# A four-layer kernel whose set-up is put in a new order: adapter rows made by full-array matmuls, first gates on ScalarE's queue, x loads and stores on SyncE

## The chip, the cores and the metric

The kernel runs on one core of a Trainium2 chip. TensorE (PE) multiplies, VectorE (DVE), ScalarE (ACT) and GpSimd (POOL) do elementwise work, SyncE (SP) only issues DMAs. The metric is the device time of one execution in microseconds. All matrices outside the recurrence are float32; the recurrent weights and state are split into two float16 parts.

## The reference

Four residual layers on x of 8 x 512 tokens of 256 channels, conditioned on 8 vectors of 256, each `x = x + layer(x)`:

```
L0: shared expert silu(x sw1') * (x sw3') @ sw2', plus 8 experts gelu(x rw1') @ rw2' weighted by the
    top-2 gates of sigmoid(x router' + cond router_t'), the sum / 3
L1: Haar transform, gated by g(cond); equals x + g * x per channel
L2: adapter: c = layernorm(cond); h = gelu(c W1 + b1); w = h W2 + b2 -> a1, b1, a2, b2, each (8, 256, rank 8)
    mid = gelu(x base_down + (x a2) b2');  out = mid base_up' + (mid b1) a1';  x + out
L3: GRU over 512 steps: Z, R = sigmoid(..), H~ = tanh(xh + (R*H) Whh'), H = Z H + (1-Z) H~, Y = H Whq'
```

W2 is 256 x 8192, 8 MB, half of all that is loaded.

## The kernel before

Tokens are time-major: a block is 16 time steps of 8 batches, 128 tokens, and there are 32 blocks. Activations lie with channels on the partitions. The loop (`blocks(body)`) runs over blocks; in block m it does the 16 recurrent steps of m, and between the steps' matmuls it places pieces of other blocks' work: output projection of m-1, layers 1 and 2 of m+1, layer 0 of m+2, the router of m+3 (`between_z_h`, `between_steps` on TensorE, `early`, `late` on VectorE, `after` on ScalarE). Every engine runs its own program in written order, and semaphores order the engines against each other. No scheduler has a say.

A block's gates go from token rows to a broadcast over partitions through DRAM: VectorE's 14 `gate_op`s end in `comb_rows`; SyncE's `spread_gates` writes them to `gates_dram` and loads them back to all partitions (`gates`); VectorE multiplies the experts' GELUs by them (`times_gate`), and TensorE's `l0_out` on `ge` and `rw2` follows. GpSimd computes the router's exponential (`exp_scores`), loads x (`load_x`, released by `x1_done`) and stores the output (`store`).

Before the loop, layer 0 of blocks 0 and 1, the router of 0 to 2 and layers 1 and 2 of block 0 must be done; this is the set-up. In TensorE's program it is: small products of cond, scores, `l0_whole_a` of block 0 (sw1, sw3, rw1), two matmuls for the scales of the recurrent weights, `l0_whole_b` of block 0 (sw2, rw2, which waits for the gates), the adapter, `l0_whole_a` of block 1, scores of block 2, then the chain of layer 2 of block 0 (`mid_base`, `low_in_rank`, `mid_low`, `up_base`, `up_low`), its projection into the gate banks (`project`), and `l0_whole_b` of block 1.

The adapter: `ah` (8 columns per half of the channels) stands in the array and W2 streams in 16 chunks of 512 columns to 8 rows of a bank; VectorE copies each chunk to `wrow`, and after each four chunks SyncE sends 8 DMAs that lay them out as `low`, (batch, rank) on 64 partitions, four such tiles: a2, b1, b2, a1. Biases are added, a2 and b1 are transposed to `a2b1`.

SyncE issues all weight loads in one row of code (L251 to L279), and only behind them `spread_gates(0)`.

## Time and profile before

| | us |
|---|---|
| median of 3 runs | 1319.07 (1315.98 to 1319.58) |
| the profiled execution | 1319.18 |
| its span | 1317.3 |
| TensorE busy | 1236.6 (94%) |
| VectorE busy | 898.1 (68%) |
| ScalarE, GpSimd busy | 444.5, 120.1 |
| first loop matmul starts | 121.96 |

The span is the stretch from the first to the last recorded instruction; the profiled execution's own time is 1.9 us more. Busy shares are means over set-up and loop, which have different limits. In the trace a float32 matmul is recorded as two instructions, and all matmuls have one line, L389, so they are told apart by tiles: `aw` is W2 (and W1 of the adapter), `rw` the routed experts or the router, `sw` the shared expert, `bank` one of four PSUM banks. SPq and POOLq are the engines' DMA issues. PEclk is the clock that TensorE was granted, 1.00 for 2.4 GHz and 0.50 for 1.2 GHz.

### The profile page before, as it was taken

The numbers are of one execution on the slowest core, as the hardware profiler recorded it, in microseconds if no ns is written. First come the engines' busy times: TensorE is split into PE (matmuls) and PEld (weight loads), VectorE is DVE, ScalarE is ACT, GpSimd is POOL, SyncE is SP. The second block draws the span as 40 slices with busy tenths as digits, with TensorE's granted clock in tenths as the row PEclk, the third lists the DMA queues.
The fourth block names the chain that finished last, engine by engine and source line by source line (L and its number), as shares of the span: only waits on it lengthen the run. The fifth ranks groups of instructions, "written<-read, shape, count | busy, mean of one in ns | idle before, by whom it ended". The sixth has DMA issues, their size and how long they took to land.

```text
span 1317.3 us, 53620 instructions
## 1 busy us (share of the span) xinstructions
PE 1236.6 (94%) x22255; PEld 1182.9 (90%) x22256; DVE 898.1 (68%) x5787; ACT 444.5 (34%) x2246; POOL 120.1 (9%) x120
## 2 busy tenths in 40 slices
PE   6387999999999999999999999999999999999975
PEld 6237999999999999999999999999999999999864
DVE  3243777777777777777777777777777777777555
ACT  1001333333333333333333333333333333333322
POOL 2410000000000000000000000000000000000000
PEclk9697999999999999999999999999999999999755
DMA  9411000011011001010111100111101100100000
GB/s 346 161 25 22 16 15 27 27 27 27 27 27 27 24 7 26 28 27 27 27 27 27 25 5 27 27 28 27 27 27 27 27 7 23 28 27 23 6 6 6
DMA packets 30325, 45.14 MB, mean 34 GB/s; under 512 B 8040, under 2 KB 24880, under 8 KB 28800
## 3 DMA queue, kind: packets, MB, share of 16 engines
q1 hardware_dynamic: 26784, 32.72, 8.7%
q0 software_dynamic: 3296, 8.98, 2.0%
q8 instruction: 174, 2.85, 0.9%
q14 instruction: 71, 0.58, 0.1%
HBM read 36.71 MB, written 4.72 MB: 31 GB/s over the span
## 4 chain that ended last, share of the span: by engine, by line
PE 88%; DVE 5%; SPq 3%; ACT 1%; issue 1%; DMA 1%; POOL 0%; DVEq 0%
PE bank L389 46%; PE gate_rh L389 31%; PE gate_z L389 10%; DVE state L984 1%; ACT rg L712 1%; DVE rhp L968 1%; DMA gates_t<-comb_rows 1%; DVE comb L842 1%; SPq L278 1%; DVE scaled L840 1%; DVE comb_rows L846 0%; SPq L271 0%; SPq L277 0%; DMA gates<-gates_t 0%; ACT hin L712 0%
## 5 line engine op out<-in xcount | busy, mean ns | idle before, releaser
L389 PEld LDWEIGHTS gate_rh<-state,whp 128*128 128x128 f16 x6144 | 233.6, 97 | 46.3 <-DVE state L984 34.3
L389 PE MATMUL gate_rh<-state,whp 128*128 128x8 f16 x6144 | 248.5, 167 | 26.7 <-DVE state L984 26.5
L712 ACT ACTIVATE rg<-gate_rh 128x16 f32<-128x16 f32 x512 | 94.2, 184 | 487.6 <-PE gate_rh L389 487.6
L389 PEld LDWEIGHTS gate_rh<-rhp,whp 128*128 128x128 f16 x6144 | 231.4, 97 | 16.2 <-DVE rhp L968 10.4
L389 PE MATMUL gate_rh<-rhp,whp 128*128 128x8 f16 x6144 | 236.6, 167 | 7.4 <-DVE rhp L968 7.4
L968 DVE SCALAR_TENSOR_TENSOR rhp<-rg,hist 128x16 f16<-128x16 f32 x512 | 89.6, 175 | 185.1 <-ACT rg L712 181.9
L389 PE MATMUL bank<-ge,rw 128*128 128x128 f32 x1024 | 165.4, 292 | 19.9 <-DVE ge L870 19.9
L389 PE MATMUL gate_z<-state,whp 128*128 128x16 f16 x4096 | 180.5, 177 | 0.0
L389 PE MATMUL bank<-xt,rw 128*128 128x128 f32 x1024 | 160.8, 292 | 6.7 <-DVE sa L851 4.8
L712 ACT ACTIVATE zg<-zsum 128x16 f32<-128x16 f32 x512 | 110.6, 216 | 166.3 <-DVE zsum L973 166.3
L978 DVE TENSOR_SCALAR zin<-zg,nsscale 128x16 f32<-128x16 f32 x512 | 124.6, 243 | 58.1 <-ACT zg L712 43.5
L984 DVE TENSOR_TENSOR_SCAN state<-zin,hin 128x32 f16<-128x32 f32 x512 | 115.1, 225 | 57.5 <-ACT hin L712 5.0
L389 PE MATMUL bank<-xt,sw 128*128 128x128 f32 x1024 | 153.6, 290 | 0.0
L389 PEld LDWEIGHTS bank<-ge,rw 128*128 128x128 f32 x1024 | 132.3, 193 | 20.1 <-DVE ge L870 20.1
L389 PEld LDWEIGHTS gate_z<-state,whp 128*128 128x128 f16 x4096 | 139.2, 96 | 0.0
L389 PEld LDWEIGHTS bank<-xt,rw 128*128 128x128 f32 x1024 | 129.8, 193 | 7.2 <-DVE sa L851 5.2
L712 ACT ACTIVATE hin<-gate_rh 128x16 f32<-128x16 f32 x512 | 95.4, 186 | 110.0 <-PE gate_rh L389 110.0
L389 PEld LDWEIGHTS bank<-xt,sw 128*128 128x128 f32 x1024 | 127.8, 194 | 0.1
L712 ACT ACTIVATE halved<-hist 128x16 f32<-128x16 f32 x512 | 106.3, 208 | 0.0
L988 DVE TENSOR_TENSOR state<-hist,state 128x16 f16<-128x16 f32 x512 | 92.1, 180 | 17.8
L986 DVE TENSOR_TENSOR_SCAN hist<-zin,hin 128x32 f32<-128x32 f32 x512 | 102.0, 199 | 1.0 <-issue 1.0
L973 DVE TENSOR_REDUCE zsum<-gate_z 128x16 f32<-128x32 f32 x512 | 93.6, 183 | 0.0
(155 smaller groups left out, 1636.5 us busy)
## 6 DMA issues: line engine op xcount, KB each, us to landing
gates<-gates_t SPq DMA_DIRECT2D x32, 512.0 KB, 5.3
aw<-in_aw SPq DMA_DIRECT2D x4, 2048.0 KB, 19.9
xt<-in_xT POOLq DMA_DIRECT2D x32, 128.0 KB, 5.6
out<-osb POOLq DMA_DIRECT2D x32, 128.0 KB, 3.6
rw<-in_rw SPq DMA_DIRECT2D x2, 1024.0 KB, 11.9
sw<-in_sw SPq DMA_DIRECT2D x3, 512.0 KB, 8.3
wh<-in_wh SPq DMA_DIRECT2D x3, 256.0 KB, 9.4
wx<-in_wx SPq DMA_DIRECT2D x3, 256.0 KB, 18.9
```

Source lines behind the costliest of these rows:

```text
L278: sp.dma_start(wq[:], a["wq"]).then_inc(wq_in, 16)
L389: return pe.matmul(o, w, x, start=start, stop=stop, skip_group_check=True)
L712: return act.activation(o, i, f, **kw)
L840: i = dve.tensor_scalar(scaled[:], ssel[:], den[:, 2:3], den[:, 1:2], ALU.mult, ALU.mult)
L842: i = dve.scalar_tensor_tensor(comb[:, 0:EXPERTS], chosen[:], den[:, 3:4], scaled[:], ALU.mult, ALU.add)
L968: dve.scalar_tensor_tensor(rhp[:, :, 0], rg[:], 1.0, old, ALU.add, ALU.mult).then_inc(rh_hi, 1)
L973: dve.tensor_reduce(zsum[:], z_now.rearrange("p a k c -> p k c a"), AX_X, ALU.add).then_inc(zsum_done, 1)
L978: dve.tensor_scalar(zin[:, :, :, 1], zg[:], -1.0, nsscale[:], ALU.add, ALU.mult)
L984: dve.tensor_tensor_scan(flat(state[:]), flat(zin[:]), flat(hin[:]), 0.0, ALU.mult, ALU.add)\
L986: dve.tensor_tensor_scan(flat(new), flat(zin[:]), flat(hin[:]), 0.0, ALU.mult, ALU.add).then_inc(st_all, 1)
L988: dve.tensor_tensor(state[:, :, :, 0], new[:, :, :, 1], state[:, :, :, 1], ALU.subtract).then_inc(st_low, 1)
```

## The change

The adapter's four tiles become two pairs (by index in W2: 2 with 1, that is a2 with b1, and 3 with 0, b2 with a1), each on 128 partitions: 64 rows of one, 64 of the other. `ah` is now a wide tile of zeros with the 8 columns in its middle. For rank r of slot s a window of 128 columns is taken in which the 8 columns stand at rows (8 s + r) * 8 of the output, and 16 ranks x 2 halves of K accumulate in one bank: the rows come out in place, with rank in the outer and batch in the inner position. `wrow`, its copies and the 32 DMAs go. `own` (the mask that keeps each token's own batch) and the bias follow the new layout, and `a2b1` is one transposed tile for both a2 and b1; `um` uses its lower 64 rows, `vm` its upper.

TensorE's order in the set-up is new. First the scores and the sw1 product, before the small products; the first adapter pair before block 0's expert output; all of block 1's layer 0 before layer 2 of block 0; the second pair within that chain. GpSimd's scaling of wx moves ahead of wqh, the exponentials of blocks 1 and 2 are placed among this work.

ScalarE issues the two gate DMAs of blocks 0 and 1. SyncE loads weights in a new order, starts with x of blocks 0 and 1, and takes over the later x loads and the stores; GpSimd keeps only the exponentials in the loop.

TensorE's program from the scales to the adapter (`gs`, `ge` and `sw`, `rw` are the expert output, `aw` and `ah` the adapter), before:

```order
L389 MATMUL gate_z<-peakd,ones 128x4 [waits peaks_dve]
L389 MATMUL bank<-gs,sw 128x128 [waits gs_done,setup_act]
L389 MATMUL bank<-gs,sw 128x128 x7
L389 MATMUL bank<-ge,rw 128x128 [waits ge47_done]
L389 MATMUL bank<-ge,rw 128x128 x7
L389 MATMUL bank<-ge,rw 128x128 [waits ge03_done]
L389 MATMUL bank<-ge,rw 128x128 x7
L389 MATMUL gate_rh<-aw,ah 8x512 [waits ad2_in2,scales_done]
```

and of the change:

```order
L379 MATMUL gate_z<-peakd,ones 128x4 [waits peaks_dve]
L379 MATMUL gate_rh<-aw,ah 128x256 [waits ad2_in2,zeroed]
L379 MATMUL gate_rh<-aw,ah 128x256 x15
L379 MATMUL gate_rh<-aw,ah 128x256 [waits ad2_in1]
L379 MATMUL gate_rh<-aw,ah 128x256 x15
L379 MATMUL bank<-gs,sw 128x128 [waits l0o_in,gs_done]
L379 MATMUL bank<-gs,sw 128x128 x7
L379 MATMUL bank<-ge,rw 128x128 [waits ge47_done]
L379 MATMUL bank<-ge,rw 128x128 x7
L379 MATMUL bank<-ge,rw 128x128 [waits ge03_done]
L379 MATMUL bank<-ge,rw 128x128 x7
```

Half of the adapter now stands ahead of the matmuls that wait for the gates (`ge47_done`, `ge03_done`).

TensorE's program at the start of layer 2 of block 0 (`x,down` is `mid_base`, `x,a2b` is `low_in_rank`), before:

```order
L389 MATMUL bank<-rw,xt 128x8 [waits x_in0,pe47_done]
L389 MATMUL bank<-rw,xt 128x8
L389 MATMUL gate_rh<-ident,low 128x64 [waits ready_dve]
L389 MATMUL gate_rh<-ident,low 128x64 x3
L389 MATMUL gate_rh<-zeros 128x512 [waits zeroed,ready_dve]
L389 MATMUL gate_rh<-zeros 128x512
L389 MATMUL gate_z<-zeros 128x512 x2
L389 MATMUL bank<-x,down 128x128 [waits x2_done,l2_in]
L389 MATMUL bank<-x,down 128x128 x3
L389 MATMUL bank<-x,a2b 128x128 [waits ready_dve]
```

and of the change:

```order
L379 MATMUL bank<-rw,xt 128x8 [waits x_in0,pe47_done]
L379 MATMUL bank<-rw,xt 128x8
L379 MATMUL bank<-x,down 128x128 [waits x2_done,x1_done,l2_in]
L379 MATMUL bank<-x,down 128x128 x3
L379 MATMUL bank<-x,a2b 128x128 [waits ready_dve]
L379 MATMUL bank<-x,a2b 128x128
L379 MATMUL gate_z<-aw,ah 128x256 [waits ad2_in3]
L379 MATMUL gate_z<-aw,ah 128x256 x15
L379 MATMUL gate_z<-aw,ah 128x256 [waits ad2_in0]
L379 MATMUL gate_z<-aw,ah 128x256 x15
L379 MATMUL bank<-um,low 128x128 [waits um_done,low_dve]
```

The transposes and the clearing of the banks leave this place, the second pair enters it.

SyncE's program in a block of the loop, before:

```order
L285 DMA gates_t<-comb_rows 128x32 [waits gates_in,gating]
L290 DMA gates<-gates_t 128x4x256 [waits ge03_done,ge47_done,comb_out]
L285 DMA gates_t<-comb_rows 128x32 [waits gates_in,gating]
L290 DMA gates<-gates_t 128x4x256 [waits ge03_done,ge47_done,comb_out]
```

and of the change:

```order
L299 DMA gates_t<-comb_rows 128x32 [waits gates_in,gating]
L303 DMA gates<-gates_t 128x4x256 [waits ge03_done,ge47_done,comb_out]
L253 DMA xt<-in_xT 128x2x128 [waits x1_done]
L294 DMA out<-osb 256x1x128 [waits out_done]
L299 DMA gates_t<-comb_rows 128x32 [waits gates_in,gating]
L303 DMA gates<-gates_t 128x4x256 [waits ge03_done,ge47_done,comb_out]
```

The x load now stands behind the gates broadcast of the block before in the same queue.

The diff, cut to its core:

```diff
-LOW_ORDER = (2, 1, 3, 0)
+PAIRS = ((2, 1), (3, 0))
+SPAN = 128
...
-        spare = (gate_rh[0], gate_z[0], gate_rh[1])
+        pair_ps = (gate_rh[1][:, 0:D], gate_z[1][:, 0:D])
...
-        score_ps = E47[:, KC * TOK:KC * TOK + EXPERTS]
+        score_ps = (E47[:, KC * TOK:KC * TOK + EXPERTS], gate_z[0][:, 0:EXPERTS])
...
         @block.sync
         def _(sp):
+            def load_x(m, par):
+                at = token_start(m)
+                sp.dma_start(xt[:, par], a["xT"][:, :, at:at + TOK]).then_inc(x_in[par], 16)
+
+            def load_aw2(i):
+                columns = slice(i * RANK * D, (i + 1) * RANK * D)
+                sp.dma_start(aw2[:, :, columns], a["aw2"][:, :, columns]).then_inc(ad2_in[i], 16)
...
             sp.dma_start(rw[:], a["rw"]).then_inc(l0_in, 16)
+            load_x((0, 0), 0)
+            load_x((0, 1), 1)
+            sp.dma_start(sw1[:], a["sw1"]).then_inc(l0w_in, 16)
             sp.dma_start(lnab[:], a["lnab"]).then_inc(ad_in, 16)
             sp.dma_start(aw1[:], a["aw1"]).then_inc(ad_in, 16)
-            sp.dma_start(sw1[:], a["sw1"]).then_inc(l0w_in, 16)
-            sp.dma_start(sw3[:], a["sw3"]).then_inc(l0w_in, 16)
-            sp.dma_start(rw1[:], a["rw1"]).then_inc(l0r_in, 16)
-            sp.dma_start(sw2[:], a["sw2"]).then_inc(l0r_in, 16)
-            sp.dma_start(rw2[:], a["rw2"]).then_inc(l0r_in, 16)
+            sp.dma_start(sw3[:], a["sw3"]).then_inc(l0w3_in, 16)
             sp.dma_start(iota[:], a["iota"]).then_inc(const_in, 16)
             sp.dma_start(rbias[:], a["rbias"].partition_broadcast(P)).then_inc(const_in, 16)
-            sp.dma_start(own[:], a["own"]).then_inc(const_in, 16)
+            sp.dma_start(rw1[:], a["rw1"]).then_inc(l0r_in, 16)
...
-            for i in LOW_ORDER:
-                columns = slice(i * RANK * D, (i + 1) * RANK * D)
-                sp.dma_start(aw2[:, :, columns], a["aw2"][:, :, columns]).then_inc(ad2_in[i], 16)
-            for b in range(B):
-                sp.dma_start(abias[b * RANK:(b + 1) * RANK], a["abias"]).then_inc(abias_in, 16)
+            load_aw2(2)
+            sp.dma_start(sw2[:], a["sw2"]).then_inc(l0o_in, 16)
+            sp.dma_start(rw2[:], a["rw2"]).then_inc(l0o_in, 16)
+            load_aw2(1)
+            sp.dma_start(abias[:], a["abias"]).then_inc(abias_in, 16)
+            sp.dma_start(own[:], a["own"]).then_inc(own_in, 16)
             sp.dma_start(down[:], a["down"]).then_inc(l2_in, 16)
             sp.dma_start(up[:], a["up"]).then_inc(l2_in, 16)
+            load_aw2(3)
+            load_aw2(0)
...
+            def store(m):
+                at = token_start(m)
+                sp.wait_ge(out_done, count(m, 1))
+                sp.dma_start(out[:, :, at:at + TOK], osb[:]).then_inc(stored, 16)
+
             def spread_gates(r):
                 sp.wait_ge(gating, GATE_OPS * (r + 1))
-                if r > 0:
-                    sp.wait_ge(gates_in, 16 * r)
+                sp.wait_ge(gates_in, 16 * r)
                 sp.dma_start(gates_dram, comb_rows[:]).then_inc(comb_out, 16)
                 sp.wait_ge(comb_out, 16 * (r + 1))
-                if r > 0:
-                    sp.wait_ge(ge47_done, r)
-                    sp.wait_ge(ge03_done, r)
+                sp.wait_ge(ge47_done, r)
+                sp.wait_ge(ge03_done, r)
                 sp.dma_start(gates[:], gates_dram.rearrange("(q e) j -> q e j", q=QUADS)[:, 0:EXPERTS]
                              .partition_broadcast(P)).then_inc(gates_in, 16)
 
-            spread_gates(0)
-            for at, i in enumerate(LOW_ORDER):
-                sp.wait_ge(wrow_dve, 4 * (at + 1))
-                for b in range(B):
-                    src = wrow[b:b + 1, at % 2].rearrange("b (r d) -> b r d", r=RANK)
-                    sp.dma_start(low[b * RANK:(b + 1) * RANK, i, :], src).then_inc(low_in[i], 16)
-
-            for r in range(1, BLOCKS):
-                spread_gates(r)
+            sp.wait_ge(x1_done, 1)
+            load_x((0, 2), 0)
+
+            def body(m, par, has_y, has_l23, has_l0, has_router):
+                if m[1] == 0:
+                    spread_gates(2)
+                if has_router:
+                    sp.wait_ge(x1_done, count(later(m, 1), 1))
+                    load_x(later(m, 3), 1 - par)
+                if has_y:
+                    store(later(m, -1))
+                if has_router:
+                    spread_gates(m[1] + 3)
+
+            blocks(body)
+            store((0, BLOCKS - 1))
+            sp.wait_ge(stored, 16 * BLOCKS)
...
         @block.gpsimd
...
+            pool.memset(ah[:], 0.0).then_inc(zeroed, 1)
...
+            pool.wait_ge(gating, 1)
+            exp_scores((0, 1))
...
+            pool.wait_ge(wx_in, 16 * 3)
+            for g in (R, Z, H):
+                pool.tensor_scalar(wx[:, g], wx[:, g], xscale[:, g:g + 1], None, ALU.mult).then_inc(wx_scaled, 1)
+            pool.wait_ge(gating, GATE_OPS + 1)
+            exp_scores((0, 2))
...
-            pool.wait_ge(x1_done, 1)
-            load_x(2 * TOK, 0)
-            exp_scores((0, 1))
-            exp_scores((0, 2))
-
             def body(m, par, has_y, has_l23, has_l0, has_router):
-                if has_l0 and not (type(m[0]) is int and m[1] + 3 >= BLOCKS):
-
-                    x_block = xcols(later(m, 3))
-                    pool.wait_ge(x1_done, count(later(m, 1), 1))
-                    load_x(x_block, 1 - par)
-                if has_y:
-                    store(later(m, -1))
                 if has_router:
                     exp_scores(later(m, 3))
...
+            def experts_up(m, par):
+                pe.wait_ge(l0r_in, 16)
+                pe.wait_ge(score_in, 2)
...
+            def adapt(p):
+                for slot in range(2):
+                    pe.wait_ge(ad2_in[PAIRS[p][slot]], 16)
+                    for r in range(RANK):
+                        for k in range(KC):
+                            at = (PAIRS[p][slot] * RANK + r) * D
+                            lead = SPAN - B - (slot * RANK + r) * B
+                            i = mm(pair_ps[p], ah[:, k, lead:lead + SPAN], aw2[:, k, at:at + D],
+                                   slot == 0 and r == 0 and k == 0, slot == 1 and r == RANK - 1 and k == KC - 1)
+                i.then_inc(adapt_pe, 1)
...
+            scores((0, 0), 0)
+            pe.wait_ge(ready_dve, 2)
+            shared_up((0, 0), 0)
+            scores((0, 1), 1, 1)
...
+            gated_up((0, 0), 0)
+            experts_up((0, 0), 0)
...
-            pe.wait_ge(setup_act, 2)
-            l0_whole_b((0, 0), 0)
-
-            pe.wait_ge(scales_done, 1)
-            for c in range(ADAPT // 512):
-                if c % 4 == 0:
-                    pe.wait_ge(ad2_in[LOW_ORDER[c // 4]], 16)
-                if c >= 3:
-                    pe.wait_ge(wrow_dve, c - 2)
-                at = LOW_ORDER[c // 4] * RANK * D + c % 4 * 512
-                for k in range(KC):
-                    i = mm(spare[c % 3][0:B, :], ah[:, k], aw2[:, k, at:at + 512], k == 0, k == KC - 1)
-                i.then_inc(adapt_pe, 1)
-            l0_whole_a((0, 1), 1)
+            pe.wait_ge(zeroed, 4)
+            adapt(0)
+            l0_whole_b((0, 0))
+            pe.wait_ge(low_dve, 1)
+            for k in range(KC):
+                i = mm(gate_rh[0][:, k * P:(k + 1) * P], low[:, 0, k * P:(k + 1) * P], ident[:], True, True)
+            i.then_inc(lowT_pe, 1)
+
+            shared_up((0, 1), 1)
+            gated_up((0, 1), 1)
+            experts_up((0, 1), 1)
+            l0_whole_b((0, 1))
             pe.wait_ge(pe47_done, 2)
             scores((0, 2), 0)
 
+            m0 = (0, 0)
+            pe.wait_ge(l2_in, 32)
+            pe.wait_ge(x1_done, 2)
+            mid_base(m0)
             pe.wait_ge(ready_dve, 4)
...
+            low_in_rank(x2, u_done)
+            adapt(1)
+            pe.wait_ge(low_dve, 2)
+            mid_low(m0)
             for t in (*gate_rh, *gate_z):
                 i = mm(t[:, :], zeros[:, 0:P], zeros[:], True, True)
             i.then_inc(bits_set, 1)
-            pe.wait_ge(l2_in, 32)
-            mid_base(m0)
-            pe.wait_ge(ready_dve, 5)
-            low_in_rank(0, x2, u_done)
-            mid_low(m0)
             up_base(m0)
-            low_in_rank(1, g2, v_done)
+            low_in_rank(g2, v_done)
...
-            l0_whole_b((0, 1), 1)
-            pe.wait_ge(split_w, 6)
+            pe.wait_ge(split_w, 5)
...
+            def comb_to_dram(r):
+                act.wait_ge(gating, GATE_OPS * (r + 1))
+                if r > 0:
+                    act.wait_ge(gates_in, 16 * r)
+                act.dma_start(gates_dram, comb_rows[:]).then_inc(comb_out, 16)
...
+            def gates_to_all(r):
+                act.wait_ge(comb_out, 16 * (r + 1))
+                if r > 0:
+                    act.wait_ge(ge47_done, r)
+                    act.wait_ge(ge03_done, r)
+                act.dma_start(gates[:], gates_dram.rearrange("(q e) j -> q e j", q=QUADS)[:, 0:EXPERTS]
+                              .partition_broadcast(P)).then_inc(gates_in, 16)
...
             gelu_experts(m0, 1, E47, ex47_done, pe47_done)
+            comb_to_dram(0)
             gelu_experts(m0, 0, A1, ex03_done, pe03_done)
+            gates_to_all(0)
+            comb_to_dram(1)
+            gates_to_all(1)
             tanh_a1(m1)
...
+            gelu_mid(m0)
             act.wait_ge(biases, 3)
             act.wait_ge(bits_set, 1)
             seed_rh(0)
             seed_z(0)
-            gelu_mid(m0)
...
+            def add_low_bias(p):
+                dve.wait_ge(adapt_pe, p + 1)
+                dve.tensor_tensor(low[:, p], pair_ps[p], abias[:, p], ALU.add).then_inc(low_dve, 1)
...
-            l0_whole_a(m0)
+            dve.wait_ge(score_exp, 1)
+            add_router_bias(m1, 1)
+            dve.wait_ge(const_in, 16 * 2)
+            gates_whole(m0)
+            silu_a1(m0)
+            times_a3(m0)
             find_scales()
...
-            l0_whole_b(m0)
+            gates_whole(m1)
+            times_gate(m0, 1, pe47_done, ge47_done)
+            times_gate(m0, 0, pe03_done, ge03_done)
+            dve.wait_ge(abias_in, 16)
+            add_low_bias(0)
             finish_l0(m0, 0)
             l1(m0)
-            for c in range(ADAPT // 512):
-                dve.wait_ge(adapt_pe, c + 1)
-                if c >= 8 and c % 4 == 0:
-                    dve.wait_ge(low_in[LOW_ORDER[c // 4 - 2]], B * 16)
-                dve.tensor_copy(wrow[:, c // 4 % 2, c % 4 * 512:(c % 4 + 1) * 512], spare[c % 3][0:B, :])\
-                   .then_inc(wrow_dve, 1)
-            l0_whole_a(m1)
+            dve.wait_ge(lowT_pe, 1)
+            dve.tensor_copy(a2b1[:].rearrange("p k c -> p (k c)"), gate_rh[0][:, 0:KC * P]).then_inc(ready_dve, 1)
+            silu_a1(m1)
+            times_a3(m1)
+            times_gate(m1, 1, pe47_done, ge47_done)
+            times_gate(m1, 0, pe03_done, ge03_done)
+            finish_l0(m1, 1)
             add_router_bias((0, 2))
             gates_whole((0, 2))
-            for i in LOW_ORDER:
-                dve.wait_ge(low_in[i], B * 16)
-            dve.wait_ge(abias_in, 16 * B)
-            dve.tensor_tensor(low[0:BR], low[0:BR], abias[:], ALU.add).then_inc(ready_dve, 1)
-            dve.wait_ge(lowT_pe, 1)
-            dve.tensor_copy(a2b1[:, :, :, 0:BR], gate_rh[0][:, 0:2 * KC * BR].rearrange("p (i k c) -> p i k c", i=2, k=KC))\
-               .then_inc(ready_dve, 1)
-            keep_own(m0, um, u_done, um_done)
-            keep_own(m0, vm, v_done, vm_done)
+            dve.wait_ge(own_in, 16)
+            keep_own(m0, um, slice(0, BR), u_done, um_done)
+            add_low_bias(1)
+            keep_own(m0, vm, slice(BR, P), v_done, vm_done)
             finish_l2(m0, 0)
-            l0_whole_b(m1)
```

## Rows read from the trace of the kernel before

**Rows 1.** The page: span, and two of the costliest groups (busy, mean ns)
```profile
span 1317.3 us, 53620 instructions
...
L389 PEld LDWEIGHTS bank<-ge,rw 128*128 128x128 f32 x1024 | 132.3, 193 | 20.1 <-DVE ge L870 20.1
...
L978 DVE TENSOR_SCALAR zin<-zg,nsscale 128x16 f32<-128x16 f32 x512 | 124.6, 243 | 58.1 <-ACT zg L712 43.5
```

**Rows 2.** TensorE by stage: stretch, length, busy (instructions), clock, DMA share, GB/s
```profile
34.00:53.60 19.60, 0.00 (x0) 0.58 0.74 241
53.60:57.00 3.40, 3.35 (x15) 0.50 0.00 0
...
95.00:105.00 10.00, 2.78 (x17) 0.67 0.21 55
...
159.50:1234.50 1075.00, 1061.77 (x20113) 1.00 0.09 24
```

**Rows 3.** Timeline: start, length; set-up matmuls for sw1 and sw3, the loop's start
```profile
13.32 5.31 PE L389 MATMUL bank<-xt,sw 128*128 128x128 f32 x32
...
121.96 0.45 PE L389 MATMUL gate_rh<-state,whp 128*128 128x8 f16 x12
```

**Rows 4.** Chain that ended last, in the set-up: start, length, what
```profile
37.76 10.11 DMA gates_t<-comb_rows
...
47.89 4.92 DMA gates<-gates_t
...
52.91 0.70 DVE ge L870
```

**Rows 5.** TensorE, adapter matmuls alone, columns as in rows 2
```profile
59.00:87.20 28.20, 27.63 (x64) 1.00 0.06 12
```

**Rows 6.** DMAs by issue: KB, us to landing; one line: landings of tile aw
```profile
sw<-in_sw SPq DMA_DIRECT2D x1, 512.0 KB, 6.6
...
xt<-in_xT POOLq DMA_DIRECT2D x1, 128.0 KB, 7.8
...
DMA to landing us min/median/max: 4.5/17.7/27.2
...
xt<-in_xT POOLq DMA_DIRECT2D x1, 128.0 KB, 2.5
...
gates<-gates_t SPq DMA_DIRECT2D x1, 512.0 KB, 5.6
xt<-in_xT POOLq DMA_DIRECT2D x1, 128.0 KB, 5.9
...
gates_t<-comb_rows SPq DMA_DIRECT2D x1, 16.0 KB, 1.4
```

**Rows 7.** VectorE in two stretches, columns as in rows 2
```profile
22.26:26.08 3.82, 3.35 (x20) 1.00 1.01 425
27.58:31.72 4.14, 2.52 (x8) 0.69 1.04 421
```

**Rows 8.** Chain, end of the set-up
```profile
109.43 0.73 PE bank L389 x4
...
113.81 1.16 PE gate_rh L389 x8
...
116.76 5.37 PE bank L389 x48
```

**Rows 9.** Timeline of a steady block, queues, VectorE and TensorE
```profile
160.74 0.37 SPq L290 DMA_DIRECT2D gates<-gates_t  x1
160.77 0.74 POOL L351 DMA_DIRECT2D xt<-in_xT  x1 [21.64 <-DVE x L888]
...
163.73 0.45 DVE L978 TENSOR_SCALAR zin<-zg,nsscale 128x16 f32<-128x16 f32 x1 [0.17 <-ACT zg L712]
...
169.84 0.59 PE L389 MATMUL bank<-rw,xt 128*128 128x8 f32 x4
```

**Rows 10.** Timeline, the last store
```profile
1314.10 0.69 POOL L356 DMA_DIRECT2D out<-osb  x1 [34.47 <-DVE osb L913]
```

174 lines of the change are left out of this document (71 added, 103 removed).

## The prediction

> **What bounds the kernel now.** I read the page first, then TensorE's busy time by stage, then the chain of waits in the set-up, then when the transfers landed, and last the timeline of one steady block.
>
> The page has a span of 1317.3 us [rows 1]. The table by stage [rows 2] splits the span: from 159.5 to 1234.5 us TensorE is busy 1061.77 of 1075.00 us at clock 1.00, so the recurrence loop is bound by TensorE, and what a queue does there can hardly shorten it. The set-up, which ends where the loop's first matmul starts, at 121.96 us [rows 3], is another matter: TensorE does nothing from 34.0 to 53.6, works at half of its clock until 57, and is busy for only 2.78 us of the ten from 95 to 105.
>
> The chain names the cause of the first hole [rows 4]: the write of the first gates to DRAM can be issued only at 37.76, behind all weight loads in SyncE's program, and takes 10.11 us to land behind them in the queue; the broadcast back takes 4.92, and VectorE's product starts at 52.91. All adapter matmuls, 27.63 us of work between 59.0 and 87.2 [rows 5], stand behind that product in TensorE's program, though the second of their four groups of weights, issued at 15.00, had landed 17.7 us later, at 32.7 (it is the median of the five `aw` loads; the first is W1's) [rows 6], and the first group before it.
>
> **The change, part by part.** The loads' bytes are nearly the same, so their landings set the earliest times. I follow TensorE's program in the new order and ask at each step which input comes last.
>
> *First stage.* sw1 was issued at 3.40 and landed 6.6 us later, at 10.0 [rows 6]; only the two x loads, which GpSimd's queue moved in those same microseconds, are new ahead of it. A 128-column f32 matmul is two instructions in the trace. 32 of them took 5.31 us in this cold stage, 0.166 each, the first ones about 0.21 [rows 3]. So 16 for sw1 (3.4), 4 for scores (0.8), 8 for l1w2 (1.7) bring VectorE its input at 15.9. With the tanh, `gate2` and the second score (1.5, my estimate from operations of 0.2 us each) its gate chain starts at 17.4. It took 3.82 us from its start to `sa` [rows 7] and `sa` some 0.6 (512 columns), so `sa` is there at 21.9 and `gs` at 22.6; TensorE, with its earlier work done by about 21, runs group 0-3 to 23.7. From the peak reductions to the end of the second tiny matmul 4.14 us passed [rows 7], so the adapter may start at 22.6 + 4.1 = 26.7.
>
> *The adapter.* Before, 8 columns of `ah` stood in the array and 512 columns streamed; now 128 stand (mostly zeros) and 256 stream. 64 instructions took 27.63 us, 0.432 for 512 columns [rows 5], so 0.216 for 256: 6.9 us for the 32 instructions of one slot, 27.6 for all 128. TensorE's work does not shrink. What the wider weight load adds is unknown. From below nothing: 48 instructions with full loads took 5.37 us, 0.112 each [rows 8], against 0.108 for the bare stream of 128 columns at the adapter's rate. From above 132.3 / 1024 = 0.129 each [rows 1], 16.5 us for 128 loads. I take nothing, as the first row has the same load under even shorter streams. Slot one ends at 26.7 + 6.9 = 33.6.
>
> The Trainium skill, page "TensorE: Matmul & The Clock Gate", section on LDWEIGHTS, has a load take its columns over 1.2 GHz: 107 ns for 128 columns. Exposed, that would be 13.7 us for 128 loads; the 0.112 us per load and stream of this trace speaks against it.
>
> *The second slot waits for its weights.* The same bytes precede them as before: 32.7 us, plus the first gates' 0.5 MB, which now travel among the loads; at the 425 GB/s of this stage [rows 7] that is 1.2 us, I take 1.3 (bounds: 0, and the 4.92 of that transfer alone [rows 4]). So 34.0; the pair ends at 34.0 + 6.9 = 40.9.
>
> *The first gates* leave on ScalarE's queue, behind a GELU released by group 4-7, at 22. For the 16 KB write the bounds are 1.4 us (in a steady block [rows 6]) and 10.11; for the 512 KB broadcast 4.92 and about 10 among the loads. The nearest row is an x load of GpSimd that landed after 7.8 us among the weights [rows 6]. I take 3 and 8: product done by 22 + 3 + 0.4 + 8 + 1.3 = 34.7, needed at 40.9 + 1.8 = 42.7. Cover: 8 us. The second gates leave when the first products are done and land by 48; they are needed near 56. Their own VectorE chain (3.8 us) stands ahead of the first product, but ends before those gates land.
>
> *Then TensorE has no hole.* Expert output of block 0, 48 instructions, 5.4: 46.3. Transposes of `low`: 46.8. Block 1's first half, 64 instructions at 0.112: 54.0. Its expert output: 59.4. x1 on VectorE: 59.9. `mid_base` and `low_in_rank`, 12 instructions: 61.2. Second pair, 64 x 0.216: 75.0. Its bias and semaphores, 0.7: 75.7; the mask `um` is ready by 66 (scores at 60, GpSimd's exponential under 2, gate chain 3.8). From `mid_low` to the first projection 109.43 to 113.81, 4.4 us [rows 8], and 0.2 for the clearing matmuls that now lie under the GELU: 80.3. 24 projection instructions, 2.7: the loop starts at 83.0. The seeding of the banks behind the GELU is done near 78.5, hidden by the chain through `vm`; GpSimd's scaling of wx starts when wx lands, near 50, and is hidden by the expert work; uncovered they would cost at most some 1 and 5 us, by my estimate.
>
> Saved in the set-up: 121.96 - 83.0 = 39.0 us, of which 19.6 are the first hole [rows 2]; the rest is the second hole with the DMA copies of `low`, time at half clock, and smaller waits.
>
> *The loop.* SyncE takes over the x load and the store. In the steady block the gates broadcast is issued at 160.74 and takes 0.37, GpSimd's x load at 160.77 and takes 0.74 [rows 9]; so the x load now starts near 161.1. Side by side they landed after 5.6 and 5.9 us, a lone x load in 2.5 [rows 6]. TensorE wants x at 169.84 [rows 9]. One behind the other, 161.1 + 5.6 + 2.5 = 169.2, still in time. While GpSimd issues its store, one VectorE operation took 0.45 us [rows 9] instead of its mean of 0.243 [rows 1]: 0.2 us in 30 blocks is 6 us at most; I take nothing, since TensorE has no gap there.
>
> *The end.* GpSimd issues the last store in 0.69 us [rows 10], SyncE issues in 0.37 [rows 9]: 0.3 less.
>
> Sum: 39.3 us. The profiled execution took 1319.18 us (the median of the runs is 1319.07): 1319.18 - 39.3 = 1279.9, forecast 1280.
>
> **Rivals.** *Gates late.* Small write 10.11 us, broadcast 10: products done at 43.8, and the second gates slip behind the end of the loads and hold block 1's experts too. Against: nothing stands ahead of them in their own queue. 3 to 9 us more: 1286. The Trainium skill ("DMA: Bandwidth & Descriptors", section "Issuing engines are not separate DMA queues") has all issuers interleave on the same 16 engines; by it the gates share, but don't wait out, the loads. No row here shows two hardware queues at once.
>
> *The change doesn't do what it says.* The gates arrive when the loads are through, as at 52.81 before. The expert product starts at 53.65 instead of 42.7 and runs its first 1.8 us of work at half clock: 12.8 us more, 1293.
>
> *Exposed weight loads.* By the upper bound up to 16.5 us: 1294, if three of the four slots pay it.
>
> *Earlier.* The cold stage warms sooner, the weights land at 32.7 and VectorE's 0.2 us a block counts: 6 to 10 us less, 1272.
>
> *Slower than before.* The x load behind the gates in one queue. If each needs its shared time in turn, x lands at 161.1 + 5.6 + 5.9 = 172.6, and TensorE waits 2.8 us in each of 29 blocks, 80 us: 1360. It decides the sign from 39.3 / 29 = 1.36 us a block, x landing after 171.2. Against: the lone load of 2.5.
>
> **How the numbers follow.** Forecast 0.67, its own range 1275 to 1284 (weights landing 1.3 earlier to 3.6 later, and some cold or warm stretch); gates late 0.12; gates after the loads 0.08; exposed loads 0.05; earlier 0.04; slower 0.03; a weaker stall that just eats the gain 0.01. The range 1273 to 1292 holds the forecast, the late gates and part of the neighbours, some 0.8. About 0.3% (4 us) is what a measurement here can tell from no change; faster 0.95, same 0.01, slower 0.04.
>
> **What would show it.** Right: the loop's first matmul at 80 to 86 us; two runs of adapter matmuls, the first from near 27 with its second half released by the DMA of `aw` near 34, the second from 61 to 75 without gaps; the first product with the gates near 34, TensorE not waiting for it; clock 1.00 from there to the loop; steady blocks as long as now (29 in some 1073 us, 37.0 each). Wrong: adapter instructions over 0.23 us apart, TensorE waiting for `ge` after 43, half clock between 34 and 60, or longer blocks with TensorE waiting for x at the scores.

## The result and the profile after

| | before | after |
|---|---|---|
| median of the runs, us | 1318.61 (1315.98 to 1319.58, 4 runs) | 1280.58 (1279.89 to 1281.78, 4 runs) |
| profiled execution; span | 1319.18; 1317.3 | 1279.89; 1277.3 |

The ratio is 0.9716, 95% interval [0.9699, 0.9732]. The forecast was 1280 in a range of 1273 to 1292.

TensorE's part of the timeline of the kernel after, from sw1's arrival to the loop (columns: start, duration, engine, line, operation, tiles, shape, count, and in brackets the idle time before it with its releaser):

```profile
10.26 3.65 PE L379 MATMUL bank<-xt,sw 128*128 128x128 f32 x16 [1.09 <-DMA sw<-in_sw]
...
22.17 2.05 PE L379 MATMUL bank<-xt,rw 128*128 128x128 f32 x16 [0.75 <-DVE sa L873]
...
26.48 15.77 PE L379 MATMUL gate_rh<-aw,ah 128*128 128x256 f32 x64
42.08 1.95 PE L379 MATMUL bank<-gs,sw 128*128 128x128 f32 x16
45.52 3.84 PE L379 MATMUL bank<-ge,rw 128*128 128x128 f32 x32 [1.49 <-DVE ge L892]
...
86.08 0.45 PE L379 MATMUL gate_rh<-state,whp 128*128 128x8 f16 x12
```

Where the kernel before had a hole of 19.6 us [rows 2] and the adapter behind it [rows 5], the first adapter pair now runs from 26.48 to 42.25, the shared half of the expert output follows without a gap, and TensorE waits 1.49 us for the gates. The loop starts at 86.08 instead of 121.96 [rows 3]: 35.9 us.

The chain of waits of the kernel after, same stretch (start, duration, what), answers to [rows 4]:

```profile
3.83 6.29 DMA sw<-in_sw
...
21.57 7.45 DMA gates_t<-comb_rows
29.04 15.63 DMA gates<-gates_t
...
44.77 0.70 DVE ge L892
...
45.52 3.84 PE bank L379 x32
...
64.45 13.83 PE gate_z L379 x64
78.30 0.43 DVE low L1101
```

The gates leave at 21.57, 16 us sooner than before, but are under way for 23.1 us (7.45 and 15.63), where the forecast had 11.4 (3, 0.4 and 8). The second adapter pair is the row of 13.83 us: 64 matmuls, 0.216 each.

TensorE's granted clock in the first pair (stretch, busy time and count, clock, DMA share, GB/s):

```profile
26.40:28.00 1.60, 1.60 (x8) 0.79 1.03 414
28.00:30.00 2.00, 2.00 (x6) 0.50 0.97 397
30.00:32.00 2.00, 2.00 (x9) 0.81 1.06 391
32.00:34.00 2.00, 2.00 (x11) 1.00 1.02 411
```

The first pair is 15.8 us and not 13.8 because the clock was at 1.2 GHz from 28 to 30 and partly so on both sides of that.

Elsewhere three things differ. In the first loop block the profiled execution of before had a half-clock stretch (granted 0.78 and 0.65 from 124 to 130 us); from the first loop matmul to the first store's issue it took 163.48 - 121.96 = 41.5 us, after takes 126.07 - 86.08 = 40.0. From the first to the 28th store's issue it is 998.2 and 996.7; all of the difference is one block of before, 38.55 us long where it is 36.94 after, with these rows in the kernel before:

```profile
602.00:605.00 3.00, 2.40 (x41) 0.76 0.04 8
605.00:608.00 3.00, 3.00 (x41) 0.67 0.65 179
```

From there to the end it is 155.6 and 154.6; in both kernels most of this runs at a granted clock of 0.50 (the last 83 us of before, nearly all of the last 84 us of after). So 35.9 + 1.5 + 1.5 + 1.1 = 40.0 us between the spans, of which the set-up, which is what the change touched, gave 35.9. The other blocks of the loop add up to the same within 0.1 us, and the list of TensorE's waits in the kernel after (releaser: us in total, times, longest) has no x in it that a DMA brings:

```profile
PE gate_rh L379 <- DVE state L1006: 26.2, 54, 0.6
PE gate_rh L379 <- DVE rhp L990: 7.4, 29, 0.3
PE bank L379 <- DMA rw<-in_rw: 4.2, 1, 4.2
PE bank L379 <- DVE ge L892: 1.5, 1, 1.5
PE bank L379 <- DMA sw<-in_sw: 1.1, 1, 1.1
```

### The profile page after: what moved, and what is told of

Same layout as the page of the kernel before. It is cut to its first block, busy times and chain, and to the rows that moved or that the text cites. A ratio compares the mean times of both kernels' runs of the same rounds, so it can differ in the third digit from the quotient of the medians.

```text
span 1277.3 us, 53686 instructions
## 1 busy us (share of the span) xinstructions
PE 1228.9 (96%) x22315; PEld 1194.4 (94%) x22316; DVE 893.7 (70%) x5772; ACT 443.9 (35%) x2246; POOL 72.8 (6%) x55
## 4 chain that ended last, share of the span: by engine, by line
PE 90%; DVE 5%; DMA 2%; ACT 1%; issue 1%; SPq 0%; DVEq 0%
PE bank L379 48%; PE gate_rh L379 31%; PE gate_z L379 11%; DMA gates<-gates_t 1%; DVE state L1006 1%; ACT rg L714 1%; DVE rhp L990 1%; DMA gates_t<-comb_rows 1%; DVE comb L864 1%; DMA sw<-in_sw 0%; DVE scaled L862 0%; DVE comb_rows L868 0%; ACT hin L714 0%; DVE zin L1000 0%; DVE rhp L997 0%
## 5 line engine op out<-in xcount | busy, mean ns | idle before, releaser
L1000 DVE TENSOR_SCALAR zin<-zg,nsscale 128x16 f32<-128x16 f32 x512 | 119.0, 232 | 57.8 <-ACT zg L714 43.4
L346 POOL TENSOR_TENSOR expn<-euler,score 128x8 f32<-128x8 f32 x32 | 52.5, 1639 | 1041.0 <-DVE score L824 1035.8
```

What stands on the lines that cost most here:

```text
L346: pool.tensor_tensor(expn[:], euler[:], score[:], ALU.pow).then_inc(score_exp, 1)
L1000: dve.tensor_scalar(zin[:, :, :, 1], zg[:], -1.0, nsscale[:], ALU.add, ALU.mult)
```

## The experiments

Ratios are to the kernel before on the same chip (the median of before in brackets). "Span" is the profiled execution's.

**First gates behind the loads again.** After, with the first two round trips issued by SyncE:

```
-            comb_to_dram(0)          (ScalarE; and gates_to_all(0), comb_to_dram(1), gates_to_all(1))
+            first_gates(0)           (SyncE, behind the last load: the same waits and DMAs)
+            first_gates(1)
```

> The changed kernel, with the two first round trips of the gates issued by SyncE behind all the loads instead of by ScalarE. Theory (the landing of the first gates bounds TensorE from 42 us on, because the adapter and the shared expert are done by then): gates_t is issued near 34 us, and with some 16 to 20 us from issue to the landing of the broadcast TensorE waits until about 50 to 55 us instead of 45.5, so +5 to +10 us, 1286 to 1291 us. Rival (the adapter covers the gates wherever they are issued, ScalarE's queue is worth nothing): 0 us, 1280.6 us. Second rival (behind the loads the round trip runs alone and takes 1.4 + 5.4 us of transfer instead of 7.45 + 15.6): lands near 43 to 45 us, 0 to -1.5 us.

1287.64 us (1316.08), ratio 0.9782 [0.9763, 0.9800]; span 1285.9, that is 8.6 more than after. The chain, and TensorE's product with the gates and its start of the loop:

```profile
31.21 15.97 DMA gates_t<-comb_rows
47.20 4.68 DMA gates<-gates_t
51.98 0.70 DVE ge L902
```

```profile
52.73 6.71 PE L393 MATMUL bank<-ge,rw 128*128 128x128 f32 x32 [10.17 <-DVE ge L902]
...
96.16 0.44 PE L393 MATMUL gate_rh<-state,whp 128*128 128x8 f16 x12
```

The gates land at 51.89 instead of 44.68, and the product with them starts at 52.73 instead of 45.52: 7.2 us later both times. Behind a wait of 10.2 us it runs mostly at half clock, 6.71 us instead of 3.84, so the loop starts at 96.16, 10.1 later than after. The span grows by less, 8.6, for reasons that lie in the loop: the first block is 1.4 us longer here (41.36 and 39.99), and the stretch from the 29th store's issue to the end, at half clock in both, 2.9 shorter. That the wait has grown by 8.7, nearly the span's 8.6, is chance. The theory holds: behind the first pair and the shared half the gates bound TensorE. The second rival falls: the small write does not run alone. It took 15.97 us for 16 KB from the same queue as the loads, issued behind them. The broadcast, issued when these are through, takes 4.68.

**The queue alone, in the kernel before.** ScalarE issues block 0's round trip, all else as before:

```
-            spread_gates(0)                                        (SyncE)
+            act.wait_ge(gating, GATE_OPS)
+            act.dma_start(gates_dram, comb_rows[:]).then_inc(comb_out, 16)
+            act.wait_ge(comb_out, 16)
+            act.dma_start(gates[:], ...partition_broadcast(P)).then_inc(gates_in, 16)
```

> The kernel before, with nothing changed but that the first round trip of the gates is issued by ScalarE as soon as the router is done (37.8 us there) and not by SyncE. Theory (the queue is one part of the gain and not the whole of it): in the kernel before the loads of the later experts are still under way, gates land at 45 to 53 us instead of 52.8, and the adapter's chain behind is unchanged, so -8 to 0 us, 1311 to 1318 us; of the 39 us of the whole change at most a fifth. Rival (the queue was the change): -30 us or more, below 1290 us. By the 23.1 us that the same two transfers took in the changed kernel beside the loads, the landing would be at 61 us and the kernel would be slower by up to 8 us.

1311.51 us (1316.08), ratio 0.9955 [0.9939, 0.9970]: 5.9 us. The chain:

```profile
25.43 7.69 DMA gates_t<-comb_rows
33.14 13.92 DMA gates<-gates_t
47.16 0.70 DVE ge L874
```

The 37.8 us of the expectation was the time at which SyncE came to issue the write; the router was done long before, and ScalarE issued it at 25.43. TensorE's wait for `ge` is 13.6 instead of 19.9 us, and the loop starts at 115.78, 6.2 us sooner. The queue is a sixth of the change's gain by itself; 12 us sooner at the start became 6 sooner at the landing.

**The adapter's place.** After, `adapt(0)` one line lower, behind block 0's expert output:

```
-            adapt(0)
             l0_whole_b((0, 0))
+            adapt(0)
```

> The changed kernel, with the first pair's adapter product moved from ahead of the first expert block to behind it (one call moved by one line). Theory (it lies under the wait for the gates): TensorE stands idle from about 26 us, but for the shared expert's part of the block, until the gates at 44.7 us, and the 13.8 to 15.8 us of the adapter come behind; +13 to +16 us, 1293 to 1297 us. Rival (its 128x256 weight loads were filling time that the first block would have used anyway; or the adapter was waiting for its weights): 0 to +3 us, 1281 to 1284 us.

1296.36 us (1316.08), ratio 0.9849 [0.9827, 0.9872]; span 1293.2, 15.9 more than after. TensorE in the stretch that the adapter filled, and its wait:

```profile
34.00:44.80 10.80, 0.00 (x0) 0.60 1.02 404
```

```profile
45.64 5.84 PE L379 MATMUL bank<-ge,rw 128*128 128x128 f32 x32 [13.56 <-DVE ge L892]
51.31 13.98 PE L379 MATMUL gate_rh<-aw,ah 128*128 128x256 f32 x64
65.88 0.71 PE L379 MATMUL gate_rh<-ident,low 128*128 128x128 f32 x4 [0.59 <-DVE low L1101]
...
102.87 0.45 PE L379 MATMUL gate_rh<-state,whp 128*128 128x8 f16 x12
```

The hole is back: TensorE waits 13.56 us for gates that land at 44.80, as in the kernel after (44.68). So the product starts only 0.1 us later. It runs longer, 5.84 us instead of 3.84, because it starts at half clock; then comes the pair with 14.0, and TensorE waits 0.6 us for `low`, whose bias no longer has the expert output to hide under. These 16.7 us are nearly all of the 16.8 by which the loop starts later, at 102.87. (The span grows by 15.9: one loop block is longer here and the last stretch shorter.) The rival falls. This one line of the order is the largest single piece of the gain that was measured.

If the 10.1 and the 16.8 us add up, they leave 9 of the set-up's 35.9 open. A likely part is the second hole, which no experiment brings back: in the kernel before TensorE waited 6.6 us for `low`, from 95.8 to 102.4, and in the kernel after it waits 0.5 us for `low` behind the second pair. That is read from the two traces; the new form of the adapter was not undone by itself.

**Stores by GpSimd.** After, only the output stores moved back to GpSimd:

```
-                if has_y: store(later(m, -1))          (SyncE)
+                if has_y: store(later(m, -1))          (GpSimd; and the last store with its wait)
```

> The changed kernel, with the stores of the output issued by GpSimd again, as in the kernel before; the loads of x stay with SyncE. Theory (who issues them touches no wait of TensorE in the steady block): 0 us, within 1 us of 1280.6 us; in each block an operation of VectorE beside the store's issue (the zin of L978 in rows 9) takes 0.45 us again instead of 0.23. Rival (the 0.2 us by which it is shorter come off each block): +0.2 us x 31 = +6 us, 1287 us.

1283.44 us (1316.57), ratio 0.9746 [0.9730, 0.9762]. That is 0.3% above after's ratio, more than the theory gave and less than the rival; the intervals overlap. The page's row of the operation, and the matmuls of the set-up:

```profile
L1000 DVE TENSOR_SCALAR zin<-zg,nsscale 128x16 f32<-128x16 f32 x512 | 124.8, 244 | 58.0 <-ACT zg L714 43.5
```

```profile
10.31 3.75 PE L379 MATMUL bank<-xt,sw 128*128 128x128 f32 x16 [1.12 <-DMA sw<-in_sw]
...
17.98 3.76 PE L379 MATMUL bank<-xt,sw 128*128 128x128 f32 x16
...
47.22 5.35 PE L379 MATMUL bank<-ge,rw 128*128 128x128 f32 x32 [3.61 <-DVE ge L892]
```

The mean is back at 244 ns, as in [rows 1] (after: 232). But from the first to the 29th store's issue this kernel takes 1163.22 - 129.56 = 1033.66 us, after takes 1159.70 - 126.07 = 1033.63: VectorE's 5.8 us more cost the loop nothing, and the rival falls. Of the 4.0 us by which the profiled execution's span is longer, 3.2 lie in the set-up, which the edit does not touch (loop start at 89.30 instead of 86.08), 0.3 in the first block and 0.5 behind the 29th store. In this execution the first matmuls stay at 0.23 us each until 23 us, in the kernel after they run at 0.13 from 14 to 17 us and again from 20; so the gates leave at 24.28 and not 21.57. The 0.5 us at the end are two unlike parts: the last blocks are 2.6 us shorter, and behind the last store's issue the execution goes on for 5.6 us instead of 2.5. Of these, GpSimd's closing drain takes 3.0 (1278.05 to 1281.06), behind the store's landing; in the kernel before it took 0.65. If it takes 3 us in every run, it is most of the 4 us by which all five lie above the forecast; one profile does not show that. The x loads were not moved back in any run, so what their move to SyncE does by itself was not separated.

**Later loads held back.** After, with one wait in SyncE's program:

```
             sp.dma_start(up[:], a["up"]).then_inc(l2_in, 16)
+            sp.wait_ge(gates_in, 16)
             load_aw2(3)
```

> The changed kernel, with SyncE waiting for the first gates to land before it issues the last adapter groups (load_aw2(3), load_aw2(0)) and all that follows. Theory (the round trip of 23.1 us is dear because its packets share the DMA engines with the loads): the gates land near 35 to 40 us instead of 44.7, TensorE's wait of 1.5 us for ge goes, -1.5 us, about 1279 us. Rival A (the loads in front are issued by then anyway and only those of before 21.6 us hold the round trip up): no change of the landing, 0 us, and the held loads come 10 us later, which nothing waits for before 64 us. Rival B (the held loads become the wait: wx is needed by 49.8, aw2 group 3 and 0 by 64): +2 to +6 us, up to 1287 us.

1277.65 us (1316.57), ratio 0.9700 [0.9683, 0.9718]; span 1275.1. The held loads leave when the gates have landed, at 36.31, so the broadcast, issued at 30.62, took 5.7 us and not 15.6:

```profile
36.31 1.20 SPq L257 DMA_DIRECT2D aw<-in_aw  x2
```

```profile
26.50 14.08 PE L380 MATMUL gate_rh<-aw,ah 128*128 128x256 f32 x64
...
42.20 3.74 PE L380 MATMUL bank<-ge,rw 128*128 128x128 f32 x32
```

TensorE no longer waits for `ge`, and the second pair finds its weights. The theory holds in the trace, rivals A and B fall. The small write still took 7.7 us; the loads that it shares with were issued by then. The product starts at 42.20 instead of 45.52: 1.5 us of this is the wait, and 1.8 the first pair, which ran at full clock in this execution and without the hold would only have waited longer. The price falls on block 1's gates: their broadcast rides with the held loads, takes 8.93 us instead of 5.65 and lands at 54.17, 1 us before TensorE reaches their product. The loop starts at 82.67, 3.4 us sooner, and loses 1.3 of it to a half-clock stretch just behind, from 86 to 90 us (clock 0.50 to 0.73). The intervals of this ratio and of after's overlap, so the gain in time is not shown by this run alone; the earlier landing is.

**Zero matmuls around the peaks**, to keep TensorE busy ahead of the adapter:

```
+            for _ in range(4): mm(gate_z[1][:, :], zeros[:, 0:P], zeros[:], True, True)
             pe.wait_ge(peaks_dve, 5)
             ...
+            for _ in range(2): mm(gate_z[1][:, :], zeros[:, 0:P], zeros[:], True, True)
             pe.wait_ge(peaks_dve, 7)
```

> The changed kernel, with six added bf16 matmuls of zeros (128x128 by 256) into a bank that nothing reads at that time, four ahead of the first peak product and two between the two, where TensorE waited for VectorE. Theory (the half clock at 28 to 30 us and the 0.8 around it follow TensorE's three waits just ahead, and cost the adapter 1.9 us; but the gates land at 44.7 us whatever the adapter does, so the gain goes into the wait for them): the first adapter product takes 13.8 to 14.2 us instead of 15.8, the wait for ge 3.4 us instead of 1.5, and the time stays at 1280.6, within 0.7 us. Rival (the adapter's end sets the block): -1.9 us, 1278.7 us. Second rival (the clock does not follow these waits): the product takes 15.8 us as before, 0 us.

1278.87 us (1316.57), ratio 0.9716 [0.9696, 0.9736], the ratio of after. The profile does what the theory says:

```profile
25.56 14.17 PE L379 MATMUL gate_rh<-aw,ah 128*128 128x256 f32 x64
...
44.44 3.84 PE L379 MATMUL bank<-ge,rw 128*128 128x128 f32 x32 [2.92 <-DVE ge L897]
```

The pair is 1.6 us shorter and the wait for the gates 1.4 longer, so a shorter adapter alone gains nothing while the gates come last. But that the fill kept the clock up is not shown: the kernels with gates on SyncE, with stores by GpSimd and with held loads have no fill and also had 14.08 us.

**Both**, held loads and the six zero matmuls:

```
+            sp.wait_ge(gates_in, 16)
+            4 and 2 matmuls of zeros, as above
```

> Both of the two edits above in the changed kernel: the last adapter groups held back until the first gates have landed, and the six added matmuls of zeros. Theory (the adapter's end and the gates' landing both bound the first block, so they pay only together): -1.5 us of the wait for ge and -1.9 us of the half clock, -3.4 us, 1277.2 us. Rival (holding loads back doesn't bring the gates forward): 0 us, as with the fill alone. Rival (held loads late at 64 us): +2 us or more.

1275.86 us (1316.57), ratio 0.9693 [0.9677, 0.9710], span 1271.6, loop start at 81.76. Against after's 0.9716 that is 0.0023 x 1317 = 3.0 us, near the expected 3.4, though the intervals overlap. The broadcast took 7.56 us here. The gates have landed when the held loads leave at 35.55, 6 us ahead of the first `ge` matmul at 41.29; a stretch at half clock right behind the loop's start is there again (granted 0.66 from 84 to 87 us).

**After once more**, nothing edited, beside the two fills below:

> The changed kernel once more, nothing edited, beside the two fills below. Theory (what differs between profiled executions in the first 30 us, the rate of the matmuls and the landing of sw1, is chance and not the kernel): ratio to before within 0.2% of 0.9716, 1277 to 1282 us; the half clock at 28 to 30 us of the first profile need not come again, and the first adapter product then takes 13.8 to 14.2 us. Rival (the half clock there belongs to the kernel): it comes again at the same place, with 15.8 us. The loop without a half-clock stretch from the first to the 29th store's issue is 1033.6 us; with one it is 1.6 us longer.

1279.45 us (1318.26; five runs from 1277.62 to 1285.67), ratio 0.9726 [0.9699, 0.9753]. The half clock came again, at the same place, and the first pair took 15.77 us again:

```profile
25.57 15.77 PE L379 MATMUL gate_rh<-aw,ah 128*128 128x256 f32 x64
...
44.66 3.84 PE L379 MATMUL bank<-ge,rw 128*128 128x128 f32 x32 [1.54 <-DVE ge L892]
```

So the theory's 13.8 to 14.2 us did not come: both profiles of this kernel have the stretch. But that it belongs to the kernel, as the rival says, does not follow. The kernel with GpSimd's stores has the same program until the loop, and its pair took 14.08 us. In both profiles with the stretch the clock had also been at half from about 17 to 20 us. Of the other kernels with the adapter in this place only the one with six zero matmuls halved there too, and it kept its fast pair, so the fill may have helped it; one profile does not show that. What brings the stretch on stays open.

Two of the five runs are 5 to 8 us above the others (1284.84 and 1285.67), so a difference of 3 us between medians of five is near the limit of what can be told.

**Zero matmuls at the start.** Seven 128x512 bf16 matmuls of zeros ahead of TensorE's first product, two ahead of sw1's:

```
+            pe.wait_ge(filled, 1)
+            for _ in range(7): mm(gate_z[1][:, :], fill[:, 0:P], fill[:], True, True)
             pe.wait_ge(cond_in, 32)
             ...
+            for _ in range(2): mm(gate_z[1][:, :], fill[:, 0:P], fill[:], True, True)
             pe.wait_ge(ready_dve, 2)
             shared_up((0, 0), 0)
```

> The changed kernel, with seven matmuls of zeros (128x512 bf16) ahead of TensorE's first product, where it waited 4 us for the first loads, and two ahead of the shared expert's first matrix. Theory (the first 128x128 products run at 0.23 us each until 13 to 22 us, twice their later 0.127, because TensorE has done little so far; so the first gates are issued at 20.7 to 24.3 us instead of below 20): sw1's 16 products take 2.03 us instead of 3.65 to 3.76, the gates are issued 1.5 to 3 us sooner and land 1 to 3 us sooner, -1 to -3 us, 1278 to 1279.5 us. Rival A (gates' transfers end with the loads beside them whatever the start): 0 us. Rival B (the slow rate at the start doesn't follow from what TensorE did): the products stay at 0.23 us, 0 us.

1280.98 us (1318.26), ratio 0.9721 [0.9700, 0.9742]. No gain that these runs can tell, and the rate at the start stayed (rival B), though TensorE was busy from 1.18 us on almost without a gap:

```profile
1.18 3.17 PE L381 MATMUL gate_z<-fill 128*128 128x512 bf16 x7 [1.18 <-DVE fill L828]
...
9.69 3.62 PE L381 MATMUL bank<-xt,sw 128*128 128x128 f32 x16
...
15.68 2.03 PE L381 MATMUL bank<-xt,sw 128*128 128x128 f32 x16
```

**All three edits:**

```
+            sp.wait_ge(gates_in, 16)
+            4 and 2 matmuls of zeros around the peaks, 7 and 2 at the start
```

> The changed kernel with all three edits: the last adapter groups held back until the first gates have landed, six zero matmuls around the peaks, nine at the start. Theory (the gates land well ahead of the adapter's end, so TensorE is bound by its own work from the arrival of sw1 on): each us of the start comes through to the end, -1.6 us or more against the hold and fill version, 1273 to 1274.5 us. Rival A (DVE's chain, not TensorE's rate, sets the start of the adapter product: 24 to 26.5 us as before): 0 to -0.5 us against it. Rival B (the slow rate does not follow what TensorE did): 0 us.

1276.05 us (1318.26), ratio 0.9682 [0.9667, 0.9698]: 3.4 us below after on the same chip (1279.45), and here the two intervals do not overlap. It is the one comparison in which holding the loads back, together with the fills, is faster than after by more than the noise. From the version with two edits it is not apart. The broadcast took 7.49 us, and block 1's gates landed so late, at 55.0, that TensorE waited 0.42 us for them. The small matmuls did start fast this time, and the clock then fell in the stretch that matters:

```profile
4.45 0.58 PE L382 MATMUL bank<-rtw,cond_tok 128*128 128x8 f32 x4
...
10.16 3.75 PE L382 MATMUL bank<-xt,sw 128*128 128x128 f32 x16 [2.06 <-DMA sw<-in_sw]
```

```profile
4.00:8.00 4.00, 3.46 (x23) 0.98 0.91 240
8.00:14.00 6.00, 3.94 (x20) 0.50 0.92 319
14.00:20.00 6.00, 5.56 (x46) 0.94 1.04 415
```

So in neither fill kernel did sw1's products run faster, once at granted clock 1.00 and once at 0.50. The fill at the start shows no gain.

## Why the prediction was right, and where its steps were not

*The bound and the holes.* Right. The gain is the set-up's: 35.9 of 40.0 us between the spans, forecast 39.0 of 39.3. The two experiments that undo one part show it on the path, by the start of the loop: the adapter behind the expert output costs 16.8 us, the gates on SyncE 10.1.

*First stage.* sw1 landed at 10.12 (forecast 10.0), the adapter started at 26.48 (26.7). Right; the gates were issued at 21.57, forecast 22. In the other executions of this order that issue lies between 20.7 and 24.3 us.

*The adapter's size.* "What the wider weight load adds ... I take nothing" held: second pair 13.83 us for 64 instructions, no gap. The rival with exposed loads is out (its own terms, 12.4 us for three slots, give 1292 and not 1294). That the first pair took 15.77 is the clock.

*"The second slot waits for its weights."* The landing was right: these weights were issued at 13.16 and landed at 34.23, forecast 34.0. The wait did not come, which changed nothing behind it. In this execution the first slot, stretched by the clock, lasted until 35.18. Where the first slot ran at full clock the weights had landed too: in the kernel with held loads at 31.48, and its second slot started at 33.51 and the pair ended at 40.6, close to the 40.9 that I had put down to a wait.

*"I take 3 and 8"*, the two terms of the first gates, were mis-sized: 7.45 and 15.63 us. I took values near the lower bound, by an x load in GpSimd's queue (7.8 us), and reasoned that nothing stood ahead of them in their own queue. That was true: the write, issued at 21.57, landed at 29.02 and so passed the adapter weights that SyncE had issued at 17.48, which landed at 42.85. It was not enough, as the loads beside them hold them up: with the later ones held back the broadcast took 5.7 to 7.6 us. VectorE's products were done at 45.5 where I had 34.7, which uses up the cover of 8 us and 2.8 more: TensorE's product starts at 45.52, forecast 42.7. So the rival "gates late" was right in its first part (it had 43.8 for the products), and the 3.1 us that the set-up lost are the lower end of its 3 to 9. Its second part did not come: no wait for block 1's gates.

By my own list two signs of being wrong were seen, TensorE waiting for `ge` after 43 us and an adapter pair with matmuls over 0.23 us apart, and the loop's first matmul, 86.08, lies just outside the 80 to 86. The time came out as forecast even so.

The Trainium skill ("DMA: Bandwidth & Descriptors", section "Issuing engines are not separate DMA queues") has all issuers interleave on the same 16 engines. The traces agree that they share: the broadcast took 15.63 us while the engines moved 404 GB/s in all, and 5.7 with the later loads held back.

*From the expert output to the loop* the forecast had 83.0 - 46.3 = 36.7 us, and it took 86.08 - 49.36 = 36.7. All of the set-up's miss of 3.1 us arose before that, and it is the gates': 2.8 in the start of the product, and 0.2 in its length. The half clock in the first pair, which ended at 42.25 and not 40.9, is no part of the sum. With a pair 1.4 us shorter TensorE would have waited 1.4 us longer for the same landing, as it did in the kernel with six zero matmuls.

*The loop.* "I take nothing" for VectorE's 0.2 us a block held: with GpSimd's stores back the loop is as long to 0.03 us. The slower rival fell: no wait for x. What I did not price is the 1.5 us in the first block and the 1.5 us in another, where the clock of before's profiled execution was low and after's not. It is not the change's. In the kernel with the queue alone, whose loop is before's, that other block took 37.17 us, and in the kernel with the adapter behind, whose loop is after's, a different block took 38.38. The first block took 41.3 to 41.4 us in four kernels with after's loop (gates on SyncE, held loads alone and with the six zero matmuls, zero matmuls at the start) and 40.0 in the others with that loop.

So the mechanism was right but for the gates' round trip, and that the sum fits the two profiled executions so closely (40.0 us between the spans, forecast 39.3) is luck, because two misses cancelled: 3.1 us too much promised in the set-up, and 4.1 us in the first block, one other block and the end, of which 0.3 had been forecast. In medians the gain is 38.0 us, 1.3 below the sum; that some of the miss is averaged away there is my reading, not shown.

*Opened by this:* once the gates are on the path, what to change is the loads beside them. Holding back what is needed only after 60 us is one wait in the program; with the fills it gave 1275.9 to 1276.1 us, the fastest versions here. What the hold gives without the fills is not shown beyond the noise.

## What to carry to other kernels

A small transfer on the critical path was not made fast here by its own queue: it passed the loads that stood ahead of it, but shared the DMA engines with them. Hold back what is not needed yet until it has landed, and look at which transfer the held loads will then meet. Before a wait on a round trip, place work whose inputs are there, and size the cover by the slow price of the round trip; a misjudged landing then costs only what exceeds the cover. A shorter piece of work ahead of such a wait gains nothing by itself. And compare set-up, loop blocks and end one by one between two traces before a difference of 1 to 3 us between their spans is given to the change: two spans can agree with a sum whose parts do not.

## What the hardware showed unexpectedly

A 16 KB write took 7.0 to 7.7 us from ScalarE's queue beside the loads, 15.97 from SyncE's behind them, and 1.4 in a steady block [rows 6]. The 512 KB broadcast took 13.9 to 15.7 us beside the loads, 5.7 to 7.6 with the later loads held back, 4.68 when the loads were through, and 5.6 in a steady block [rows 6].

The first 128x128 f32 matmuls run at 0.23 us each while the granted clock in the profile's rows is 1.00, and later at 0.127 at the same granted clock; the change of rate came between 12.5 and 14.3 us in six executions, near 17 in the two kernels with before's order, and between 21.5 and 23 in three. The row of the granted clock does not show it; only the durations do. The slow rate is that of half clock: sw1's 16 products took 3.75 us where they were slow from first to last, and 3.75 in the one execution where the row did say 0.50. What sets the time of the change was not found: seven added matmuls at 1 to 4 us left it at 14 us in one kernel, and in another brought fast matmuls at 4.5 us and half clock from 8 to 14.
